# Score and max products over all 128 rows of the array, with rows 100 to 127 filled with zeros

## The reference, cut to what matters

```python
xn = _layernorm(x)
qkv = jnp.einsum('bsd,de->bse', xn, W_qkv)            # q, k, v: 16 heads of 32
attn = jnp.einsum('bhqd,bhkd->bhqk', q, k) / sqrt(32)
attn = softmax(attn + alibi_bias + causal_mask)        # slope_h * (j - i) for j <= i
y = jnp.einsum('bhqk,bhkd->bhqd', attn, v)  ...  @ W_o
# experts: logits = xn @ wg; idx = argmax; gate = softmax(logits)[idx]
out = x + y + gate * (xn @ W[idx].T + b[idx])
```

## Time and profile before

| | us |
|---|---|
| median of 3 runs | 1939.15 |
| lowest, highest | 1935.37, 1945.24 |
| span of the profiled execution | 1937.1 |

### The profile page before, as it was taken

The page is one execution under the profiler, slowest core; times in us unless marked ns, Lnnn a source line. Parts: engine busy times, 40 slices in busy tenths (PEclk is TensorE's granted clock), DMA queues, the critical chain, the costliest instruction groups (busy, mean ns, idle before and its releaser), DMA issues. The chain is left out here.

```text
span 1937.1 us, 31890 instructions
## 1 busy us (share of the span) xinstructions
PE 1789.7 (92%) x10482; PEld 1023.6 (53%) x10483; DVE 1131.4 (58%) x2001; ACT 913.7 (47%) x1575; POOL 665.3 (34%) x665
## 2 busy tenths in 40 slices
PE   5999999589699999999999999999999999789798
PEld 4777777344344444444444444444444443478687
DVE  5433334577487577666665667767766670344366
ACT  3222222055356566565565566656656567621211
POOL 6000000067152452442444246245244346211260
PEclk9999999588899899999899899999989999899999
DMA  6667744959508205502700900730450230244496
GB/s 229 220 216 261 266 168 147 163 204 252 64 7 145 32 7 104 68 14 58 114 8 9 169 8 7 139 39 7 99 72 8 76 116 12 104 152 163 145 390 240
DMA packets 102350, 227.81 MB, mean 118 GB/s; under 512 B 9832, under 2 KB 27240, under 8 KB 96648
## 3 DMA queue, kind: packets, MB, share of 16 engines
q1 hardware_dynamic: 87648, 176.20, 36.3%
q0 software_dynamic: 14560, 49.75, 7.0%
HBM read 128.47 MB, written 96.93 MB: 116 GB/s over the span
## 5 line engine op out<-in xcount | busy, mean ns | idle before, releaser
L1061 ACT ACTIVATE probs_sb<-score_ps,bias 128x512 f32<-128x512 f32 (+3 forms) x1280 | 733.1, 624 | 506.2 <-PE score_ps L1129 303.7
L975 DVE TENSOR_REDUCE part_max<-max_ps 128x1 f32<-128x512 f32 (+3 forms) x1280 | 722.0, 603 | 394.5 <-PE max_ps L1091 203.0
L959 POOL TENSOR_TENSOR pair_sum<-probs_sb 128x512 f32<-128x512 f32 x384 | 479.8, 1281 | 592.5 <-ACT probs_sb L1061 592.3
L1126 PE MATMUL score_ps<-q_aug,k_aug 100*128 100x512 f32 (+3 forms) x1280 | 531.1, 422 | 42.3 <-ACT probs_sb L1061 24.4
L1091 PE MATMUL max_ps<-k_aug,q_aug 98*128 98x512 f32 (+3 forms) x1280 | 523.6, 421 | 40.1 <-DMA q_aug<-q_rows_d 33.4
L1126 PEld LDWEIGHTS score_ps<-q_aug,k_aug 100*128 100x128 f32 x1280 | 251.3, 197 | 305.9 <-ACT probs_sb L1061 231.5
L1091 PEld LDWEIGHTS max_ps<-k_aug,q_aug 98*128 98x128 f32 x1280 | 260.2, 204 | 181.7 <-DVE part_max L975 104.7
L1170 PE MATMUL acc_ps<-probs_sb,v_sb 128*32 128x512 f32 (+3 forms) x2560 | 308.6, 555 | 0.0
L1010 DVE RECIPROCAL acc_sb<-acc_sb 128x128 f32<-128x128 f32 x128 | 119.6, 939 | 74.0 <-ACT acc_sb L1043 74.0
L618 DVE SCALAR_TENSOR_TENSOR st_lo<-group_ps,st_hi 128x512 fp32r<-128x512 f32 x64 | 44.3, 692 | 139.1 <-ACT st_hi L665 138.4
L1094 PE MATMUL max_ps<-mask_qk,ident_bf 128*128 128x128 bf16 x512 | 124.3, 243 | 0.0
(11 more groups left out here) (177 smaller groups left out, 1684.5 us busy)
## 6 DMA issues: line engine op xcount, KB each, us to landing
k_aug<-k_hi_d SPq DMA_DIRECT2D x14, 1024.0 KB
q_aug<-q_hi_d SPq DMA_DIRECT2D x14, 1024.0 KB
slot_x_d<-zero_f POOLq DMA_DIRECT2D x20, 512.0 KB, 7.1
rows<-slot_x_d SPq DMA_DIRECT2D x40, 256.0 KB, 2.6
slot_y_d<-y_rows POOLq DMA_DIRECT2D x39, 256.0 KB, 2.5
xn_d<-xn SPq DMA_DIRECT2D x8, 1024.0 KB, 9.9
q_hi_d<-st_hi SPq DMA_DIRECT2D x32, 256.0 KB, 7.7
q_lo_d<-st_lo SPq DMA_DIRECT2D x32, 256.0 KB, 7.6
```

The source lines that it names most:

```text
L959: nc.gpsimd.tensor_tensor(pair_sum[:, p % 2, hh], probs[:, s0, hh], probs[:, s1, hh], ALU.add).then_inc(pair_added, 1)
L975: nc.vector.tensor_reduce(part_max[:, hh * QT + i, kc:kc + 1], max_ps[:, bank, 0:w], AX.X, ALU.max).then_inc(max_taken, 1)
L1061: nc.scalar.activation(probs[:, r % P_SLOTS, hh, off:CH], score_ps[:, (r * HG + hh) % S_BANKS, off:CH], ACT.Exp, bias=bias[:, half, hh * Q ...
L1126: last = nc.tensor.matmul(score_ps[:, u % S_BANKS, off:CH], k_aug[0:ROWS, half, hh, jb * P:(jb + 1) * P], q_aug[0:ROWS, half, hh, cc * CH ...
```

## The change

Both products run over all 128 partitions. Rows 100 to 127 of both operands are filled by DMA with zeros, read from row 2 of q_rows_d and repeated over the 28 partitions: once for each half, in group 0 chunk by chunk ahead of each chunk's load, and in group 1 behind the wait for the slots. Later groups leave them as they are. The waits for the loads count the added transfers.

```diff
+PAD_ROWS = P - ROWS
+        pad_zeroed = [sem("pad_zeroed0"), sem("pad_zeroed1")]
+        PADS = 16 * 2
...
+                def zero_pad(half, here, zeroed):
+                    zeros = m.q_rows_d[2][:, here].partition_broadcast(PAD_ROWS)
+                    for aug in (k_aug, q_aug):
+                        sp.dma_start(aug[ROWS:P, half, :, here].bitcast(F32), zeros).then_inc(zeroed, 16)
...
                     if isinstance(g, int) and g == 1:
 
                         sp.wait_ge(slots_stored, 16 * NT)
+                        zero_pad(half, slice(0, S), pad_zeroed[half])
                     if isinstance(g, int) and g == 0:
 
                         for cc in range(QC - 1):
+                            zero_pad(half, slice(cc * CH, (cc + 1) * CH), first_loaded[cc])
                             load_qk(g, half, slice(cc * CH, (cc + 1) * CH), first_loaded[cc])
...
                     if isinstance(g, int) and g == 0:
+                        zero_pad(half, slice(S - CH, S), pad_zeroed[half])
                         load_qk(g, half, slice(S - CH, S), aug_loaded[half])
...
-                    last = nc.tensor.matmul(max_ps[:, bank, 0:w], q_aug[0:ROW_MAX, half, hh, i * P:(i + 1) * P],
-                                            k_aug[0:ROW_MAX, half, hh, kc * CH:kc * CH + w], start=True, stop=not diag)
+                    last = nc.tensor.matmul(max_ps[:, bank, 0:w], q_aug[:, half, hh, i * P:(i + 1) * P],
+                                            k_aug[:, half, hh, kc * CH:kc * CH + w], start=True, stop=not diag)
...
+                            if isinstance(g, int) and g == 0:
+                                pe.wait_ge(pad_zeroed[1], PADS)
...
-                            pe.wait_ge(first_loaded[1], AUG)
+                            pe.wait_ge(first_loaded[1], AUG + PADS)
...
                             pe.wait_ge(aug_loaded[0], AUG)
+                            pe.wait_ge(pad_zeroed[0], PADS)
...
-                    last = nc.tensor.matmul(score_ps[:, u % S_BANKS, off:CH], k_aug[0:ROWS, half, hh, jb * P:(jb + 1) * P],
-                                            q_aug[0:ROWS, half, hh, cc * CH + off:(cc + 1) * CH], start=True, stop=not diag)
+                    last = nc.tensor.matmul(score_ps[:, u % S_BANKS, off:CH], k_aug[:, half, hh, jb * P:(jb + 1) * P],
+                                            q_aug[:, half, hh, cc * CH + off:(cc + 1) * CH], start=True, stop=not diag)
...
-                        pe.wait_ge(first_loaded[2], AUG)
+                        pe.wait_ge(first_loaded[2], AUG + PADS)
...
-                pe.wait_ge(first_loaded[0], AUG)
+                pe.wait_ge(first_loaded[0], AUG + PADS)
```

## The result

The changed kernel takes 1947.19 us (median of 18 runs, 1943.76 to 1950.13), the kernel before 1940.11 us in the same session (18 runs, 1935.37 to 1950.43). The ratio is 1.0032, 95% interval [1.002, 1.0043]: 6.2 us slower (3.9 to 8.3). That is within the 0.5% that the prediction took as no change, though these runs can tell it from zero.

What follows compares the result with a forecast made beforehand. TensorE was taken to set the pace in attention, with its waits for the loads of groups 0 and 1 on the path. Pads 11.0 + 10.2, products 0: 1939.15 + 21.2 = 1960 us, range 1947 to 1976.

Steps and rivals of the forecast that it cites:

- The bound and the places: TensorE sets the pace in attention; the lengthened loads are on the path only at its waits between 340 and 520 us.
- The pads' price: Zero loads ahead of group 0's first score and group 1's opening product: 11.0 and 10.2 us, together 21.2 us.
- The rates of 167 and 180 GB/s: Pad transfers of groups 0 and 1: neighbours' 191 and 206 GB/s times 28/32, for 28 partitions written.
- Rivals 1 and 2: Pads' loads: beside other transfers at 353 GB/s, 10.4 us, chance 0.12; or crawling at 46 GB/s, 51 us, 0.10.
- The longer operands: Max and score products reading 128 rows instead of 98 and 100: 0 for 2560 products, bounds -20 to +20 us.
- rival 3: TensorE's granted clock in attention, 0.97, rises: at most 33 us back, 1927 us; decides above 21 us; chance 0.04.
- Zero rows do not shorten that: At the clock's fall at 641 us: zero rows leave TensorE's 3.33 us idle time behind ScalarE as it is.
- The lower end of the range: 1947 us for the whole kernel, taken as the case of pads beside other transfers less the spread of the runs.
- rival 1: Pads of groups 0 and 1 run beside surrounding transfers at 353 GB/s: 10.4 us, 1949.5 us; chance 0.12.

Runs made afterwards that it cites:

- e6: The kernel before plus pads issued on SP behind group 0's last shift rows; products still read 98 and 100 rows: 1.0001 times the kernel before.
- e10: The changed kernel, but only group 0's program reads 128 rows, groups 1 to 7 read 98 and 100: 1.0086 times the kernel before.
- e1: The changed kernel with its pads and waits, but all products read 98 and 100 rows again: 1.0079 times the kernel before.
- e7: The kernel before, but GpSimd instead of SP issues the store of y, on its own queue: 0.9856 times the kernel before.

## Why the prediction was wrong

**The bound and the places: right.** TensorE's waits for the loads of groups 0 and 1 are where the pads cost, and nothing is added elsewhere: e6, with the pads away from these two places, is at 1.0001. The first max product was put at 356.8 and stands at 356.60. TensorE's wait for the operand loads was put at about 46 us and came to 52.3: the idle time before the product that opens group 1's maxima is 28.08 us, not 26, and a third wait, inside group 0's load, grew to 4.9 us, which the later wait for the shift rows swallows.

**The pads' price: right in kind, somewhat too large.** Group 0: 11.0 us forecast, 9.15 in the trace; group 1: 10.2 forecast, 9.6; together 21.2 against 18.8. One trace is not exact to 2 us: in that of e10, which runs the same program up to this product, it stands 21.1 us later than before. The medians say less than 21.2, 15 us for e1 (11 to 19) and 17 us for e10 (0.0086, 14 to 20). The rates of 167 and 180 GB/s, scaled down by 28/32, were too low. While the pads of group 1 run, DMA share and GB/s are at the right of this window:

```profile
471.00:479.00 8.00, 7.98 (x43) 3.44 (x42) 7.41 (x13) 4.90 (x9) 7.00 (x7) 1.00 0.95 191
```

191 GB/s is the rate of the 32-row neighbours in the earlier trace rows, not 28/32 of it, though below the 206 GB/s of the earlier trace rows. 3.67 MB at 191 GB/s are 19.2 us. The estimate by the Trainium skill (page "SBUF — State Buffer", "Door 1: The DMA port swizzle"), 7 ports or 190 GB/s, agrees with this window; its 19.3 us lie between the two traces and nearer to the medians than 21.2. Rivals 1 and 2 are excluded by the same row.

**The longer operands: the step that failed.** "I take 0 for the 2560 products" holds for the product by itself: medians and starts are what they were. It fails for the stage, which got 10.5 us shorter by the trace and 9 to 10 by the ratios. The larger part is that of rival 3, the clock, but not as it was put there: the clock does not stay up, it comes back sooner. Of the "at most 33" us of granted clock some 7 return, after the six stalls, and another 2.3 us come from the two waits behind VectorE, which no rival had. The prediction had the pieces: the low stretch at 641 us and the real idle time ahead of it. It concluded "Zero rows do not shorten that" from the fact that the stall is not shortened, though the cost of a stall is its length and the low stretch behind it, and only the first was reasoned about. What it could not read from any row it priced at nothing ("What a full operand would have done there no row can show"), in place of a bound. With 10.5 us for this term the sum would have been 10.7 us, 1950 us. It also asked rival 3 to return over 21 us before it counted at all; half of that was enough to halve the forecast.

**The sum.** 21.2 us forecast; -2.4 by the pads' price, -7.3 at the stalls, -2.3 at the two waits, -0.9 spread over attention and -0.1 behind it make the 8.2 us of span. The median ratio says 6.2, interval 3.9 to 8.3. The lower end of the range was added up wrongly: rival 1 at 1949.5 less the spread of the runs below their median, 3.8 us, is 1945.7, not 1947.

**What stays open.** Why rows of zeros count for the clock; only zeros were tried. What makes VectorE's instruction short or long at the two waits, and why the rows of TensorE's products decide it. Whether anything of the effect lies in group 0: in the traces of the sessions where before takes 1953 us or more, a low stretch near 405 to 430 us appears with short rows in group 0, and it is missing from the traces of the other sessions, where group 0 had wide rows, but also from that of before. Rows and session can't be told apart there; by the ratios it is nothing.

## What to carry to other kernels

The price of a stall on TensorE is its length plus the stretch at 1.2 GHz behind it: here some 4 us of waiting, then 3 to 14 us at half speed. Taking five of the six stalls away (a small store moved off the queue on which megabytes of loads stand) gave 28 us, filling up the contraction rows 9 us, and both together little more than the first. And where a gain is found by a sum over a stage, follow one instruction through both timelines: the lag shows at which places the time goes, and here it showed a second cause. Zeros that fill up an operand are worth having only if they arrive where no one waits: the same 3.67 MB cost 15 us or more ahead of the loads and nothing behind them.

## What the runs showed of the hardware

The granted clock fell at each of the six stalls of 3.3 us or more, and at five places where e7 has no stall it did not fall. That an idle gap costs the clock is what the Trainium skill says ("TensorE: Matmul & The Clock Gate", part 1), and the trace agrees; six traces also have a short fall beside a wait of 0.99 to 1.00 us. Not expected: how soon the clock returns goes with the rows that the products use. Over six stalls the time at 1.2 GHz is 51 to 58 us with 98 and 100 rows and 31 to 34 us with 128 rows of which 28 hold zeros, at one spacing of the products. Nor was it expected that a VectorE instruction on 128x16 elements takes 0.17 us in one kernel and 1.35 us in the other at the same place of the program. In group 0 the clock of the changed kernel also came back between the stalls, 0.97 and 0.99 in the first two windows here (of after), where the kernel before stayed at 0.50 (last fence):

```profile
362.00:365.60 3.60, 2.12 (x10) 1.17 (x9) 3.53 (x8) 0.00 (x0) 0.00 (x0) 0.97 1.02 193
386.00:389.50 3.50, 0.77 (x4) 0.30 (x3) 2.18 (x6) 0.00 (x0) 0.00 (x0) 0.99 0.93 196
```

```profile
360.00:368.00 8.00, 6.71 (x21) 4.06 (x20) 6.55 (x14) 0.00 (x0) 0.00 (x0) 0.50 1.10 175
```

Transfers set the pace of that stage in both kernels. Up to the first score nothing was gained by it: that starts at 401.21 us in the changed kernel and at 401.54 in e1, with the same pads and short rows.
